# Forty gathers in place of fifty-four ahead of the first stores, and four in place of two after each expert's stores

## The reference, cut to what matters

```python
h = frames(x) @ dct.T                          # (32, 938, 128)
h = h + causal_convolution(layernorm(h))       # by FFT in the reference
z = layernorm(h).reshape(30016, 128)
probs = softmax(z @ Wr, axis=0)                # over the rows, 8 experts
vals, idx = top_k(probs.T, 1024)               # 1024 rows for each expert
hid = gelu(z[idx] @ W1 + b1)                   # 128 -> 512
out_e = hid @ W2 + b2                          # 512 -> 128
h = h + zeros.at[idx].add(vals * out_e)        # rows may be chosen by several experts
```

## Time and profile before

| | us |
|---|---|
| median of 3 runs | 578.6 |
| lowest and highest | 576.7, 583.95 |
| span of the profiled execution | 605.3 |
| POOL busy, and its share of the span | 298.7, 49% |
| PE busy | 397.3, 66% |
| DVE busy | 425.8, 70% |
| first gather, last gather (start) | 362.53, 546.96 |
| first store, last add (start) | 459.38, 595.93 |

### The profile page before, as it was taken

One profiled execution on the slowest core, in us unless ns is written; L12 is line 12 of the kernel. 1 busy time (PEld: TensorE's weight loads), 2 busy tenths in 40 slices (PEclk: granted clock), 3 DMA queues, 4 the chain that ended last, 5 costly groups with the idle time before them and its releaser, 6 DMA issues.

```text
span 605.3 us, 11347 instructions
## 1 busy us (share of the span) xinstructions
PE 397.3 (66%) x3577; PEld 320.0 (53%) x3577; DVE 425.8 (70%) x1653; ACT 292.2 (48%) x560; POOL 298.7 (49%) x213
## 2 busy tenths in 40 slices
PE   5798898999888889997000033210199989997900
PEld 5786788865877788764000022110057667775700
DVE  3877878898488887898888878911787658866100
ACT  2787840076699740177545500120258667686400
POOL 0467830058478730076000007776235687888774
PEclk9999999999899999999555555555579989999965
DMA  8679606699888227699999501121011344443332
GB/s 162 132 183 272 150 15 162 142 253 241 194 148 148 58 48 157 201 275 254 323 318 318 190 0 44 49 52 48 17 28 61 67 74 67 65 75 44 31 30 22
DMA packets 86116, 77.44 MB, mean 128 GB/s; under 512 B 15022, under 2 KB 82930, under 8 KB 85810
## 3 DMA queue, kind: packets, MB, share of 16 engines
q1 hardware_dynamic: 68674, 64.52, 41.6%
q0 software_dynamic: 10368, 8.40, 9.8%
q10 hardware_dynamic: 7024, 3.89, 2.7%
HBM read 52.27 MB, written 39.39 MB: 151 GB/s over the span
## 4 chain that ended last, share of the span: by engine, by line
PE 32%; DVE 21%; issue 14%; DMA 10%; POOL 10%; ACT 6%; another core or an unknown queue 5%; SPq 1%; ACTq 1%; DVEq 0%; POOLq 0%
PE banks L1003 7%; POOL out L1843 7%; PE banks L1030 5%; PE banks L929 5%; PE banks L1133 4%; PE banks L1146 4%; PE banks L1040 3%; DMA xin<-in_x 3%; ACT xn L680 2%; PE banks L915 2%; DMA ring<-toeplitz 2%; DVE xn L1512 2%; DMA const<-constants 1%; DVE xn L1576 1%
## 5 line engine op out<-in xcount | busy, mean ns | idle before, releaser
L1829 POOL DMA_INDIRECT hid<-kept,index x64 | 65.0, 1015 | 115.6 <-DVE index L1624 97.0
L1214 DVE BATCH_NORM_STATS2 stats<-hid 120x6 f32<-120x128 f32 (+1 forms) x512 | 104.9, 278 | 19.8 <-ACT hid L671 19.4
L1843 POOL DMA_INDIRECT out<-hid,index x56 | 88.6, 1582 | 25.9 <-issue 16.3
L929 PE MATMUL banks<-const,xt 128*120 128x128 f32 x512 | 74.0, 290 | 12.0 <-ACT xt L666 11.5
L775 ACT ACTIVATE xt<-banks 128x480 f32<-128x480 f32 x64 | 36.3, 570 | 84.9 <-PE banks L1030 83.7
L929 PEld LDWEIGHTS banks<-const,xt 128*120 128x120 f32 x512 | 63.9, 192 | 20.7 <-ACT xt L666 14.4
L1751 POOL TENSOR_TENSOR small<-small,powers 120x16 f32<-120x16 f32 (+2 forms) x18 | 47.9, 2662 | 47.1 <-DVE small L1232 47.1
L1819 POOL TENSOR_TENSOR small<-small,powers 120x16 f32<-120x16 f32 x15 | 43.2, 2901 | 41.7 <-DVE small L1232 36.3
L1003 PE MATMUL banks<-xn,ring 122*120 122x128 f32 x512 | 58.9, 276 | 6.3 <-DMA xn<-s 3.1
L1146 PEld LDWEIGHTS banks<-w_ring,xn 128*128 128x128 f32 x512 | 60.5, 196 | 3.9 <-issue 3.9
L1003 PEld LDWEIGHTS banks<-xn,ring 122*120 122x120 f32 x512 | 57.6, 189 | 7.4 <-issue 6.9
(11 more groups left out here) (222 smaller groups left out, 705.1 us busy)
## 6 DMA issues: line engine op xcount, KB each, us to landing
kept<-out SPq DMA_DIRECT2D x1, 15008.0 KB, 50.5
xin<-in_x SPq DMA_DIRECT2D x28, 480.0 KB, 6.9
out<-hid SPq DMA_DIRECT2D x14, 960.0 KB, 11.1
w_ring<-in_L_ffn_W SPq DMA_DIRECT2D x16, 256.0 KB
ring<-toeplitz SPq DMA_DIRECT2D x32, 112.5 KB
toeplitz<-ring SPq DMA_DIRECT2D x6, 545.0 KB, 11.3
out<-hid SPq DMA_DIRECT2D x2, 784.0 KB
xin<-in_x SPq DMA_DIRECT2D x4, 384.0 KB
```

The source lines that it names most:

```text
L929: mm = pe.matmul(banks[0:L, 2 + n % 4, i * D:(i + 1) * D], xt[:, n % 2, i, :], cut["basis_t"], start=True, stop=True)
L1214: ins = dve.bn_stats(stats[:, slot, b, :], hid[:, bass.ds(c * HB + b, 1), :].rearrange("p a k -> p (a k)"))
L1829: pool.indirect_dma_start(found[:, n, :], None, kept, bass.IndirectOffsetOnAxis(ap=index[:, n:n + 1], axis=0)).then_inc(found_in[e], 16)
L1843: pool.indirect_dma_start(rows, at_rows, adds[:, n, :], None, compute_op=ALU.add, oob_is_err=True, bounds_check=ROWS * FRAMES - 1).then_in ...
```

## The change

Two constants are changed. `FOUND_FIRST` says how many gathers POOL issues before `add(0)`, `FOUND_BETWEEN` how many at most after each `add(e)`, until all 64 are issued.

```diff
-FOUND_FIRST = 54
+FOUND_FIRST = 40
 WEIGHED_AFTER = {3: (3, 5), 5: (5, 7), 6: (7, 8)}
-FOUND_BETWEEN = 2
+FOUND_BETWEEN = 4
```

## The result

The changed kernel takes 601.79 us (median of 3 runs, 599.83 to 602.91) against 578.6 before: a ratio of 1.038, 95% interval 1.030 to 1.046. It is 23.2 us slower; 24.4 was forecast. A second build of the same code gave 601.94 against 578.3 (1.044, 1.040 to 1.048).

What follows compares the result with a forecast made beforehand. POOL was taken to bound the tail. To the median of 578.6 us came 12.4 us of POOL's queue and 12.0 us of waiting for the chain, +24.4 in sum: 603.0 us, range 589 to 612.

Steps and rivals of the forecast that it cites:

- The last gather's place: POOL's tail: the last gather starts behind expert 5's adds, at 576.96 us, 30.0 us later than before.
- The wait behind it: POOL ahead of expert 6's adds: a new wait of 12.0 us for `answer(6, 0)`, released by DVE L1694.
- The queue's term: POOL's tail: 12 more gathers among the adds, less the pauses they fill, add 12.4 us.
- What makes up the wait: DVE's queue: `answer(6, 0)` stands behind expert 7's statistics, which need the last gather; POOL waits 12.0 us.
- POOL only: Rival: DVE could answer expert 6 before needing expert 7's rows, leaving only the queue's 12.4 us; 591.0 us, chance 0.10.
- The covers: Tail: `answer(7, 0)` comes 3.3 us before POOL wants it; expert 5's and 6's later work stays covered, price 0.
- The front: Before the first stores: 14 fewer gathers give back nothing, price 0, with 0 to -2.7 us as bounds.
- two signs of being wrong: First stores clearly earlier and expert 1's adds with them, or no POOL wait before expert 6's adds.
- Long gathers: Rival: gathers beside working DVE slow down, one of 2.84 us per group, 9.3 us in all; 612 us, chance 0.03.
- Slow clock: Rival: TensorE stays at half clock through expert 7's products, the end 12 us later; 615 us, chance 0.04.
- Front bound: Rival: the gathers in front delay the tail before, so the change regains at most 17.5 us; 585.5 us, chance 0.08.
- Profile against median: Between 394 and 426 us: three unexplained DVE waits, 28.2 us, inferred absent from timed runs; difference added to the median.

Runs made afterwards that it cites:

- e9: Kernel before plus a hold on POOL: gather 32 waits until DVE has written expert 5's row numbers; 578.17 us against 578.3.
- e8: The changed kernel (40 in front, four between) built again unedited; 601.94 us against 578.3 for the kernel before.
- e11: Changed kernel with five gathers between instead of four, last gather ahead of expert 5's adds; 590.73 us against 577.62 for the kernel before.
- e3: Changed kernel with expert 7's moments and score on DVE moved between `answer(6, 0)` and `answer(6, 1)`; 624.85 us against 605.15 for the kernel before.
- e4: Changed kernel with both expert 6 answers ahead of expert 7's moments on DVE, and its second down product ahead of expert 7's transposes on PE; 596.33 us.
- e10: Changed kernel plus a hold on POOL: gather 32 waits for expert 5's row numbers; 600.11 us against 578.3 for the kernel before.
- e0: Kernel before, unedited, profiled once more; 606.08 us against 605.15 for the kernel before on that chip.
- e2: Changed kernel with five gathers between instead of four, on the chip with the unexplained waits; 617.83 us against 605.15 for the kernel before.
- e1: Changed kernel with 44 gathers in front instead of 40, four between; 617.68 us against 605.15 for the kernel before.

## Why the prediction was right

**The last gather's place.** Right, and nearly its size: 30.0 us later were forecast. From expert 1's adds the sum has 100.8 us and the trace 99.6; in the kernel before (e9) that stretch is 70.9, so the shift is 28.7.

**The wait behind it.** Right: 12.0 forecast, 11.96 found beyond the usual 0.30, 11.9 in e8, at the place, with the releaser named. e11 takes it away by where the gathers stand, with as many in front and as many among the adds.

**The queue's term.** 12.4 forecast, 11.4 in the traces. The 12 gathers cost 14.9 us instead of 15.6, and the 40 adds between took 0.6 us less in all than in e9. e11 pays the term without the other: 13.1 by the medians.

**What makes up the wait.** Half right. The prediction lays it on DVE's order and says, in *POOL only*, that without that order 12.4 us would remain. e3 shows that the wait then moves to the later adds, and with DVE's order and PE's both changed (e4) 17.6 us remain. Expert 7's own chain is the deeper reason: 28.6 us from the last gather's start to `answer(7, 0)`. The cover of 3.3 us that the prediction found at expert 7's first add existed only because POOL had just waited 12 us at expert 6's.

**The covers.** `answer(7, 0)` came 2.07 us ahead of POOL, 1.2 after the usual 0.9, where 3.3 were forecast. The chain from the last gather took 28.6 us instead of the 26.2 of the profile before; the half clock, for which the prediction had 2.5 us, is what changed in it (5.77 us against 3.74 for the down product, 1.12 against 0.66 for the transposes). It cost nothing at the end. In e9 the chain takes 27.5, part of it at half clock already. Expert 6's late statistics (9.4 us of waiting) cost nothing either.

**The front.** Wrong in kind, and small: taken as 0, with -2.7 as the bound, -3.4 in the traces. The 54 gathers lasted longer than the 1.25 us that I used for all, and the first store came 74.05 us after the first gather (e9) rather than 71.4. In e9 `answer(1, 0)` is done at 441.61 and POOL comes to it at 448.10: expert 1's adds had been held by POOL, not by DVE. The prediction found 1.1 us of waiting for DVE there because the profile before has a fourth wait with an unknown releaser, the 4.22 us ahead of `answer(1, 0)`, which it took for the program's own and which e9 doesn't have. The first stores 5.4 us earlier, and expert 1's adds with them, are one of the two signs of being wrong that the prediction names. It did appear, and only its size leaves the sum standing.

**The other rivals.** *Long gathers*: the 24 gathers among the adds took 0.97 us each on the mean, none over 1.03 (one of 1.52 us in e8, one of 1.54 in e10). The longest of the 40 in front, of 2.84, 1.85 and 2.38 us, began at 367.94, 386.45 and 406.48, beside DVE's scans of 367.86, 385.39 and 405.95. The rule that the prediction quotes for this rival fits these rows; the last scan is over before the first store, so it had no part in the tail. *Slow clock*: it is full again in the window from 562. *Front bound*: 3.4 us of it are real, of the 12.8 that it needed.

**The end.** Not in the sum: from the last add's start to the end of the span it takes 11.0 us in the changed kernel, 9.3 in e9 and 9.4 in the profile before. That adds 1.7 us, 1.6 of them in the closing drain of POOL's queue, which comes behind the last landing: 7.25 us against 5.62. Sum of the traces: -3.4 + 23.7 + 1.7 = 22.0 us; the medians differ by 23.2 and 23.6. The other 1 to 2 us can't be placed by single executions: the start of the first gather alone varies by 8 us between the profiles. That 24.4 lies so near 23.2 is in part luck, since the front (-3.4) and the queue (-1.0) were too high and the end (+1.7) was missing.

**Profile against median.** The inference that the timed runs lacked the 28.2 us was right as far as the later runs tell: kernels before that take 578 us have none of these waits (e9). It is what made 578.6 + 24.4 the right sum. The prediction gives no reason for it, and my first one, that the waits were one execution's, was wrong (e0).

## What to carry to other kernels

When one queue issues both the loads of the later steps and the stores of the earlier ones, find the last load and follow its chain to the last store that needs it: a load may slip only as far as the slack at the end of that chain. Here the place behind one more block of stores (15.5 us) cost 10 us. Such a move had two terms here, what the queue pays for every load put among the stores and what it waits for the slipped chain; a variant that moves only the last load tells them apart. A wait that an in-order queue shows at one instruction may be only the first of several for the same event, so reordering that queue moves it instead of removing it.

## What the runs showed that I had not expected

- The same program takes 605 us on one chip and 578 on the others. With the 605 us go waits of DVE's ahead of L1614, 28.1 us in e0, in three pieces, while gathers are in flight. The third ended 5.8 to 5.9 us after the start of the last gather in the row (420.11 and 417.59: 425.95 and 423.48) with 44 in a row, and 5.2 us after it with 40 (414.51 and 419.75 in e2, 410.18 and 415.40 in e3). With 40 it was 4.6 us long in e2 and 6.7 in e3, with 44 10.2 in e1. One more such wait, ahead of `answer(1, 0)`, is 4.2, 6.9 and 8.3 us long with two, four and five gathers behind the first stores. That they hang on gathers in flight is what these rows suggest; the kernels meant to test it (e9, e10) fell on chips without them, and why one chip has them stays open. The experiments have one such chip, and its four programs ran together, so that the waits go with the chip and not with something else about those runs is not shown either.
- The stretch from the last add's start to the end of the span depends on the constants: 9.3 to 9.4 us with 54 and two, 9.9 with 54 and four, 10.3 to 11.1 in the others. What differs is the closing drain of POOL's queue, the same to the nanosecond in kernels with the same constants on any chip: 5.615 us with 54 and two, 6.268 with 54 and four, 6.595 with 44 and four, 6.922 with 48 and four and with 52 and three, 7.248 with 40 in front. These go in steps of 0.327 us, or two of them. What sets it stays open.
